# Order of scans, output product and gate in the state-space stage of a hybrid kernel

## The chip, the cores and the metric

The kernel runs on one core of a Trainium2 chip. The metric is the device time of one execution in microseconds, from runs on the chip; lower is better. The core has a matmul engine (TensorE, PE in the profile, with its weight loads shown as PEld), a vector engine (VectorE, DVE), a scalar engine for activations (ScalarE, ACT), a general engine (GpSimd, POOL) and a queue for DMAs (SyncE, SP). Each engine runs its own queue of instructions, and they synchronize by semaphores.

## The reference

Sixteen sequences of 512 tokens, 128 channels wide, pass through four residual layers: attention, a mixture of experts, a state-space layer, and the mixture of experts again. Only the state-space layer matters here. Cut to what counts:

```
zxbcdt = layernorm(x) @ in_proj_w.T        # z: 256, x: 256, B: 128, C: 128, dt: 32 heads
z, xBC, dt = split(zxbcdt);  dt = softplus(dt + dt_bias);  A = -exp(A_log)
xBC = silu(causal_conv4(xBC) + conv_b);  X, B, C = split(xBC)
# chunks of 32 tokens, 32 heads of 8 channels, state of 128
Y_diag = C B^T * exp(segsum(A dt)) applied to X dt          # within a chunk
states = B, decay to the chunk's end, X dt                  # one state per chunk
states = scan over the 16 chunks with the chunk decays
Y_off  = C applied to the state before the chunk, * exp(cumsum(A dt))
y = Y_diag + Y_off
y = layernorm(y) * ln_w * silu(z)
x = x + y @ out_proj_w.T
```

## The kernel before

The whole of `x` stays in on-chip memory. The stage runs over the sequences b = 0 to 15 (`ssm_pairs` writes out the first and last two and loops over pairs between them). Every engine has a function `batch(b, par, left)`, whose order of calls is written out by hand; it is the order of that engine's queue. `left` is the number of sequences still to come, capped at 2, and `has_before(b)` holds for all but b = 0. Within one `batch(b)` an engine does parts of three sequences: b itself, the output of b - 1, and the projections of b + 1 (with the layer norm of b + 2).

The 32 heads are taken in 8 groups of 4 (`SG` = 8). The steps named below:

- `diff(b, g)` (TensorE, L1640 to L1642): the log decays of head group g in PSUM bank g % 2. `exp_diff` (ScalarE, L1992) takes their exponential into a ring of four `decay` tiles. `mix(b, g)` (VectorE, L1838) multiplies by C B^T. `in_chunks(b, g)` (TensorE, 32 matmuls at L1668) multiplies with X and writes into banks 2 and 3.
- `fills` (TensorE, L1655) makes the chunk states in banks 6 and 7, and `fill_out` (ScalarE, L2001) copies them to `state`. `scan(b, part)` (VectorE, two instructions at L1846 for each of the parts 0 to 3) runs the recurrence over chunks. Part 0 waits for all of `fill_out`; the last scan raises `scanned`.
- `in_proj(b + 1, ..., q, back)` (TensorE, L1572 to L1574, three matmuls): convolution tap `back` of the projection of block q (0 and 1 are X, 2 is B, 3 is C), into bank 4 + q. So B goes to bank 6 and C to bank 7.
- `gate(b)` (TensorE, L306 to L308, 12 matmuls): the projection of z, into banks 0 and 1. `silu_z(b)` (ScalarE, L2017) applies Silu and raises `z_done`.
- `y_turn(b - 1)` (TensorE, L1675) transposes the previous y into banks 6 and 7, `y_copy` (ScalarE, L2010) copies it out and raises `yt_done`. `out_proj(b - 1)` (TensorE, 16 matmuls at L1682) writes the output product into bank 7. `out_add(b - 1)` (VectorE, four instructions at L1856) adds it to `x` and raises `x_done`.
- `shift_vector(b + 2)` (VectorE, L1359) makes the layer norm's shift; `norm(b + 2)` (ScalarE, four instructions at L1929) waits for it. In ScalarE's queue the order is `exp_diff(7)`, `y_copy(b - 1)`, `norm(b + 2)`, `silu_z(b)`, then `silu_x(b + 1, q)` (L1945).
- `from_state(b)` (TensorE, L1703 and L1706): C times the state, into banks 0 and 1. It waits for `z_done` and for `scanned`. After it comes `y_join(b)` (VectorE, L1866 and L1874), and with it the head of the next sequence.

The order at the end of a sequence on TensorE:

```python
                in_chunks(b, SG - 2)
                if has_before(b):
                    out_proj(b - 1)
                in_chunks(b, SG - 1)
                gate(b, par)
```

Of the kernel before, what the change touches and what calls it, by code (L numbers as in the profile page):

```python
# [35 lines left out]
TAPS, CH = 4, 32  # L36
# [37 lines left out]
def program(nc, x_in, out, w, x_slot, y_tok, phases):  # L74
    ctx = ExitStack()
    with ctx:
# [227 lines left out]
        def mm3(pe, o, a_h, a_l, b_h, b_l):  # L304

            pe.matmul(o, a_h, b_h, start=True, stop=False)  # L306
            pe.matmul(o, a_l, b_h, start=False, stop=False)
            return pe.matmul(o, a_h, b_l, start=False, stop=True)  # L308
# [366 lines left out]
        def has_before(b):  # L675
            return not (isinstance(b, int) and b == 0)
# [870 lines left out]
        FILLS = NC // 2  # L1547
# [10 lines left out]
        def ssm_tensor(pe, ph):  # L1558
# [8 lines left out]
            def in_proj(b, par, q, back):  # L1567
                k = TAPS - 1 - back
                c = slice(q * P, (q + 1) * P)
                o = bank[4 + q][:, :]  # L1570
                h, l = [x_pad[par][:, i, TAPS - back:TAPS - back + L] for i in range(2)]
                pe.matmul(o, wx_h[:, k, c], h, start=(back == 0), stop=False)  # L1572
                pe.matmul(o, wx_l[:, k, c], h, start=False, stop=False)
                last = pe.matmul(o, wx_h[:, k, c], l, start=False, stop=(back == TAPS - 1))  # L1574
                if back == TAPS - 1:
                    last.then_inc(s["xbc_mm"], 1)
# [7 lines left out]
            def sums(b):  # L1584
                pe.wait_ge(s["a_done"], b + 1)
                pe.wait_ge(s["act_x"], b * XB + 2)
                for c in range(CT):
                    last = pe.matmul(bank[5][:, :].rearrange("p (t c h) -> p c t h", t=QT, c=CT)[:, c, :, :],
                                     in_chunk[:, c, :], a_tok[:, :, :], start=True, stop=True)
                last.then_inc(s["tot_mm"], 1)  # L1590
                pe.matmul(bank[4][:, 0:P], later[:, :], flat_t(a_tok), start=True, stop=True)
                pe.matmul(bank[4][:, P:2 * P], until[:, :], flat_t(a_tok), start=True, stop=True).then_inc(s["dec_mm"], 1)
# [67 lines left out]
            def in_chunks(b, g):  # L1660
                if g == 0:
                    pe.wait_ge(s["xd_act"], b + 1)
                    pe.wait_ge(s["xd_dve"], b + 1)
                pe.wait_ge(s["mix_done"], b * SG + g + 1)
                for t in range(QT):
                    for c in range(CT):
                        o = bank[2 + t // 2][c * CH:(c + 1) * CH, (t % 2) * DI + g * CH:(t % 2) * DI + (g + 1) * CH]
                        last = pe.matmul(o, decay[:, g % D_RING, t, c, :], x_diag[:, t, c, g, :], start=True, stop=True)  # L1668
                last.then_inc(s["yd_mm"], 1)

            def y_turn(b):
                pe.wait_ge(s["y_zmul"], b + 1)
                for q in range(DI // P):
                    for t in range(QT):
                        last = pe.transpose(bank[6 + q][:, t * P:(t + 1) * P], y[:, t, q * P:(q + 1) * P], ident[:, :])  # L1675
                last.then_inc(s["yt_mm"], 1)
# [9 lines left out]
            def gate(b, par):  # L1686
                pe.wait_ge(s["diff_exp"], b * SG + SG)
                for t in range(QT):
                    c = slice(t * P, (t + 1) * P)
                    last = mm3(pe, bank[t // 2][:, (t % 2) * DI:(t % 2 + 1) * DI], xh[par][:, c], xl[par][:, c],  # L1690
                               wz_h[:, 0:DI], wz_l[:, 0:DI])
                    if t % 2:
                        last.then_inc(s["z_mm"], 1)
# [15 lines left out]
            def batch(b, par, left):  # L1709
                sums(b)  # L1710
                turns(b)
                rows(b, par, left)
                b_and_c(b)
                for g in range(SG):
                    diff(b, g)
                    if 2 <= g < 2 + QT:
                        fills(b, g - 2)
                    if left:
                        if g == 0:
                            pe.wait_ge(s["e_done"], b * 2 + 2)  # L1720
                        if g == TAPS:
                            pe.wait_ge(s["tot_done"], b + 1)
                        in_proj(b + 1, 1 - par, g // TAPS, g % TAPS)
                    if g >= 2:
                        in_chunks(b, g - 2)
                    if g == 6 and has_before(b):
                        pe.wait_ge(s["fill_out"], b * FILLS + FILLS)
                        y_turn(b - 1)
                in_chunks(b, SG - 2)
                if has_before(b):  # L1730
                    out_proj(b - 1)
                in_chunks(b, SG - 1)
                gate(b, par)
                if left:
                    if not has_before(b):
                        pe.wait_ge(s["fill_out"], FILLS)
                    for back in range(TAPS):
                        in_proj(b + 1, 1 - par, 2, back)
                    if has_before(b):
                        pe.wait_ge(s["x_done"], ph * SEQS + b)  # L1740
                    for back in range(TAPS):
                        in_proj(b + 1, 1 - par, 3, back)
                from_state(b)
                if left > 1:
                    pe.wait_ge(s["act_x"], (b + 1) * XB + 3)
                    ln_turn_wide(b + 2)
# [15 lines left out]
        def ssm_vector(dve, ph):  # L1762
# [70 lines left out]
            def mix(b, g):  # L1833
                if g == 0:
                    dve.wait_ge(s["cb_done"], b + 1)
                dve.wait_ge(s["diff_exp"], b * SG + g + 1)
                m = decay[:, g % D_RING, :, :, :].rearrange("p t c l -> p (t c l)")
                dve.tensor_tensor(m, m, cb[:, :], ALU.mult).then_inc(s["mix_done"], 1)  # L1838

            def scan(b, part):  # L1840
                if part == 0:
                    dve.wait_ge(s["fill_out"], b * FILLS + FILLS)
                    dve.wait_ge(s["tot_done"], b + 1)
                for x in range(2 * part, 2 * part + 2):
                    line = state[:, x, :, :].rearrange("p h c -> p (h c)")
                    last = dve.tensor_tensor_scan(line, e_tot[:, :, :].rearrange("p h c -> p (h c)"), line, 0.0, ALU.mult,  # L1846
                                                  ALU.add)
                if part == HP // 2 - 1:
                    last.then_inc(s["scanned"], 1)

            def out_add(b):
                dve.wait_ge(s["so_mm"], b + 1)
                dve.wait_ge(s["y_pow"], b + 1)
                for t in range(QT):
                    xt = tile_x(b * QT + t)
                    last = dve.scalar_tensor_tensor(out=xt, in0=bank[7][:, t * D:(t + 1) * D], scalar=y_rstd[:, t:t + 1],  # L1856
                                                    in1=xt, op0=ALU.mult, op1=ALU.add)
                last.then_inc(s["x_done"], 1)
# [19 lines left out]
            def batch(b, par, left):  # L1878
                scale_x(b)
                cumt_low(b)  # L1880
                cum_low(b)
                if left:
                    dt_in(b + 1)
                spread_x(b)
                if has_before(b):
                    y_moments(b - 1)
                if left:
                    dt_inverse(b + 1)
                mix(b, 0)
                mix(b, 1)  # L1890
                if has_before(b):
                    y_gate(b - 1)
                mix(b, 2)
                if left > 1:
                    ln_stats_vector(dve, SEQS + b + 2, b + 2)
                mix(b, 3)
                mix(b, 4)
                mix(b, 5)
                scan(b, 0)
                scan(b, 1)  # L1900
                mix(b, 6)
                scan(b, 2)
                mix(b, 7)
                scan(b, 3)
                if left > 1:
                    shift_vector(dve, b + 2)
                if has_before(b):
                    out_add(b - 1)
                y_join(b)
                if left > 1:  # L1910
                    ln_lo_wide_vector(dve, b + 2, par)
# [465 lines left out]
```

## Time and profile before

| | |
|---|---|
| runs, median of 3 | 2785.82 us (2782.82 to 2787.51) |
| profiled execution, its own time | 2776.01 us |
| its span | 2774.2 us |
| state-space stage, about | 1530 to 2294 us of the span |
| mean granted TensorE clock | 0.905 |
| TensorE / VectorE / ScalarE / GpSimd busy | 88% / 71% / 53% / 47% |

In the rows of a timeline the first number is the start in us from the span's start and the second how long the group took; engine, line, operation, the tile written and those read, the shape and the count follow. In brackets stands how long the engine had been idle before, and which engine, tile and line ended that wait. Instructions of an engine overlap a little at their ends, and the ends of matmuls are modelled. PEclk is the granted clock of TensorE: 1.00 is 2.4 GHz and 0.50 is 1.2 GHz. A sequence is here counted from the start of its `from_state`, so the stretch from 1703.5 to 1749.6 us ends with that of sequence 4.

### The profile page before, as it was taken

The numbers are of one execution on the slowest core, as the hardware profiler recorded it, in microseconds if no ns is written. First come the engines' busy times: TensorE is split into PE (matmuls) and PEld (weight loads), VectorE is DVE, ScalarE is ACT, GpSimd is POOL, SyncE is SP. The second block draws the span as 40 slices with busy tenths as digits, with TensorE's granted clock in tenths as the row PEclk, the third lists the DMA queues.
The fourth block names the chain that finished last, engine by engine and source line by source line (L and its number), as shares of the span: only waits on it lengthen the run. The fifth ranks groups of instructions, "written<-read, shape, count | busy, mean of one in ns | idle before, by whom it ended". The sixth has DMA issues, their size and how long they took to land.

```text
span 2774.2 us, 62048 instructions
## 1 busy us (share of the span) xinstructions
PE 2428.7 (88%) x21968; PEld 1784.7 (64%) x21968; DVE 1959.3 (71%) x5809; ACT 1469.9 (53%) x2778; POOL 1296.4 (47%) x1816
## 2 busy tenths in 40 slices
PE   4999999999999969979974999999999977988991
PEld 3666555665556548868863666666667656886881
DVE  3887888878888748856656566676666657885666
ACT  1555555555555546645552556565555646654550
POOL 0444455445544437766652324242333305774661
PEclk9999999999999986769996899999989987768996
DMA  7443444334443301113332000000000000112336
GB/s 161 63 59 49 59 59 59 56 51 59 59 59 53 42 29 47 47 56 89 91 100 83 2 2 2 2 2 2 2 2 2 2 2 29 48 51 78 91 89 192
DMA packets 118421, 140.68 MB, mean 51 GB/s; under 512 B 21452, under 2 KB 79953, under 8 KB 118000
## 3 DMA queue, kind: packets, MB, share of 16 engines
q1 hardware_dynamic: 101232, 102.68, 19.9%
q0 software_dynamic: 16896, 34.12, 3.6%
q8 instruction: 181, 2.97, 0.5%
q14 instruction: 112, 0.92, 0.1%
HBM read 45.85 MB, written 40.54 MB: 31 GB/s over the span
## 4 chain that ended last, share of the span: by engine, by line
PE 52%; DVE 19%; issue 10%; POOL 9%; ACT 7%; DMA 2%; SPq 1%; DVEq 0%; POOLq 0%; ACTq 0%
DVE state L1846 4%; POOL probs_t L562 3%; PE psum L1655 3%; POOL acc L568 3%; PE psum L476 3%; PE psum L1219 3%; DVE x_sb L1393 3%; PE psum L543 2%; PE psum L582 2%; PE psum L1193 2%; PE psum L1194 2%; PE psum L1703 2%; PE psum L1195 2%; PE psum L653 2%; DVE psum L485 2%
## 5 line engine op out<-in xcount | busy, mean ns | idle before, releaser
L485 DVE CUSTOM_DVE_ANT_0 psum<-psum,causal 128x512 f32<-128x512 f32 (+3 forms) x1024 | 481.7, 512 | 148.6 <-PE psum L476 145.5
L553 ACT ACTIVATE probs_t<-psum 128x512 f32<-128x512 f32 (+1 forms) x768 | 388.8, 523 | 356.8 <-PE psum L543 355.8
L562 POOL TENSOR_SCALAR_AFFINE_SELECT probs_t<-probs_t 128x256 f32<-128x256 f32 x512 | 189.8, 407 | 455.8 <-ACT probs_t L553 455.8
L1328 POOL DMA_INDIRECT y_tok<-yb,xb x272 | 265.8, 977 | 161.8 <-issue 128.0
L476 PE MATMUL psum<-ls,qs 96*128 96x512 f32 (+3 forms) x1024 | 323.8, 359 | 10.0 <-DVE mx_raw L485 6.3
L543 PE MATMUL psum<-qs,ls 98*128 98x512 f32 (+3 forms) x1024 | 311.9, 348 | 4.4 <-ACT probs_t L553 2.4
L476 PEld LDWEIGHTS psum<-ls,qs 96*128 96x128 f32 x1024 | 182.5, 194 | 185.3 <-DVE mx_raw L485 88.4
L996 POOL DMA_INDIRECT x_slot<-pay,pos_i x256 | 254.2, 993 | 93.3 <-issue 74.3
L2071 POOL TENSOR_SCALAR dt_r<-dt_v 128x128 f32<-128x128 f32 x16 | 9.2, 576 | 438.5 <-DVE dt_v L1767 438.5
L543 PEld LDWEIGHTS psum<-qs,ls 98*128 98x128 f32 x1024 | 177.7, 192 | 42.4 <-ACT probs_t L553 29.1
L1292 DVE TENSOR_TENSOR bh<-psum,bs 128x512 f32<-128x512 f32 x136 | 94.1, 692 | 139.2 <-ACT bs L1254 135.2
L601 PE MATMUL psum<-probs_t,lat_tok 128*32 128x512 f32 (+3 forms) x2048 | 177.8, 443 | 0.0
L568 POOL TENSOR_TENSOR acc<-probs_t 128x512 f32<-128x512 f32 x128 | 163.9, 1281 | 10.7
L1846 DVE TENSOR_TENSOR_SCAN state<-e_tot,state 128x512 f32<-128x512 f32 x128 | 148.7, 1212 | 20.7 <-ACT state L2001 20.7
L1838 DVE TENSOR_TENSOR decay<-decay,cb 128x512 f32<-128x512 f32 x128 | 95.1, 756 | 87.8 <-ACT decay L1992 87.8
L1254 ACT ACTIVATE bs<-psum 128x512 f32<-128x512 f32 x136 | 81.3, 598 | 136.7 <-PE psum L1195 136.7
L1219 PE MATMUL psum<-w_d,ht_h 128*128 x544 | 143.8, 341 | 1.2 <-DVE ht_l L1297 1.2
L2001 ACT ACTIVATE state<-psum 128x512 f32<-128x512 f32 (+1 forms) x128 | 120.0, 1046 | 45.3 <-PE psum L1655 45.3
L485 DVE DVE_READ_ACCUMULATOR2_ANT mx_raw<- 128x1 f32 x1024 | 142.4, 139 | 0.3
L1221 PE MATMUL psum<-w_d,ht_l 128*128 x544 | 121.4, 223 | 0.0
L1193 PE MATMUL psum<-w_gu_h,xt_h 128*128 x272 | 120.9, 444 | 0.2 <-issue 0.2
L1992 ACT ACTIVATE decay<-psum 128x512 f32<-128x512 f32 x128 | 74.5, 595 | 83.7 <-PE psum L1642 81.9
(336 smaller groups left out, 6805.5 us busy)
## 6 DMA issues: line engine op xcount, KB each, us to landing
qs<-q_h SPq DMA_DIRECT2D x96, 256.0 KB, 5.4
xb<-x_slot SPq DMA_DIRECT2D x272, 66.0 KB
y<-y_tok SPq DMA_DIRECT2D x32, 512.0 KB, 3.5
qs<-q_l SPq DMA_DIRECT2D x48, 256.0 KB, 5.6
qs<-r_h SPq DMA_DIRECT2D x32, 256.0 KB, 6.2
y_tok<-yb,xb POOLq DMA_INDIRECT x272
x_sb<-in_x SPq DMA_DIRECT2D x16, 256.0 KB, 5.4
qs<-r_l SPq DMA_DIRECT2D x16, 256.0 KB, 5.7
```

The lines of the kernel that those rows point to most:

```text
L476: last = pe.matmul(o[:, at:at + w_q], qs[0:3 * LD, h, qt * P:(qt + 1) * P], ls[b % 2][0:3 * LD, 0:w_q], start=(at == 0), stop=True, skip_g ...
L485: last = dve.tensor_tensor_reduce(out=bank[n % 3][:, at:at + w_q], in0=bank[n % 3][:, at:at + w_q], in1=causal[:, L - w_q:L], scale=1.0, s ...
L543: last = pe.matmul(o[:, at:at + L - kb * P], ls[b % 2][0:3 * LD + 2, kb * P:(kb + 1) * P], qs[0:3 * LD + 2, h, kb * P:L], start=(at == 0), ...
L553: act.activation(probs_t[:, i % 2, h % HG, UNIT_AT[k]:UNIT_AT[k] + UNIT_COLS[k]], bank[3 + m % 2][:, 0:UNIT_COLS[k]], ACT.Exp).then_inc(s[ ...
L562: last = pool.affine_select(out=p[:, :, at:at + P], in_=p[:, :, at:at + P], compare_op=ALU.is_ge, fill=0.0, base=0, pattern=[[0, 2], [1, P ...
L568: pool.tensor_tensor(acc[:, heads, :], p[:, :, 768:1024], p[:, :, 1024:1280], ALU.add).then_inc(s["p_step"], 1)
L601: last = pe.matmul(bank[5][j * LD:(j + 1) * LD, kb * P:L], lat_tok[b % 2][:, kb, :], probs_t[:, i % 2, j, at:at + L - kb * P], start=(kb = ...
L996: pool.indirect_dma_start(out=x_slot[f][:, :], out_offset=bass.IndirectOffsetOnAxis(ap=pos_i[slot][:, k, t:t + 1], axis=0), in_=pay[slot][ ...
L1193: pe.matmul(o, xt_h[par][:, c], w_h, start=True, stop=False)
L1219: pe.matmul(o, ht_h[par][:, m * P:(m + 1) * P], flat_d[c][:, bass.ds(at[k], 2 * D)], start=(k == 0 and c == 0), stop=False, skip_group_che ...
L1328: pool.indirect_dma_start(out=y_tok[f][:, :], out_offset=bass.IndirectOffsetOnAxis(ap=xb[:, j2, k, D:D + 1].bitcast(I32), axis=0), in_=yb[ ...
L1846: last = dve.tensor_tensor_scan(line, e_tot[:, :, :].rearrange("p h c -> p (h c)"), line, 0.0, ALU.mult, ALU.add)
```

## The change

On TensorE, the gate and the projection of B for the next sequence now come before the output product of the previous sequence; the last `in_chunks` follows the output product, and the projection of C follows that. The projection of B gets a wait for `yt_done`, because it overwrites bank 6, from which `y_copy` reads. The projection of C still waits for `x_done`, because it overwrites bank 7.

On VectorE, the last two `mix` come before all scans, `out_add` comes between scan 1 and scan 2, and the shift between scan 2 and scan 3.

```diff
@@ ssm_tensor, batch
                 in_chunks(b, SG - 2)
-                if has_before(b):
-                    out_proj(b - 1)
-                in_chunks(b, SG - 1)
                 gate(b, par)
                 if left:
-                    if not has_before(b):
+                    if has_before(b):
+                        pe.wait_ge(s["yt_done"], b * 2)
+                    else:
                         pe.wait_ge(s["fill_out"], FILLS)
                     for back in range(TAPS):
                         in_proj(b + 1, 1 - par, 2, back)
+                if has_before(b):
+                    out_proj(b - 1)
+                in_chunks(b, SG - 1)
+                if left:
                     if has_before(b):
                         pe.wait_ge(s["x_done"], ph * SEQS + b)
                     for back in range(TAPS):
@@ ssm_vector, batch
                 mix(b, 5)
+                mix(b, 6)
+                mix(b, 7)
                 scan(b, 0)
                 scan(b, 1)
-                mix(b, 6)
+                if has_before(b):
+                    out_add(b - 1)
                 scan(b, 2)
-                mix(b, 7)
-                scan(b, 3)
                 if left > 1:
                     shift_vector(dve, b + 2)
-                if has_before(b):
-                    out_add(b - 1)
+                scan(b, 3)
                 y_join(b)
```

## Rows read from the trace of the kernel before

**Rows 1.** The page, part 1: busy time and share of each engine.
```profile
...
PE 2428.7 (88%) x21968; PEld 1784.7 (64%) x21968; DVE 1959.3 (71%) x5809; ACT 1469.9 (53%) x2778; POOL 1296.4 (47%) x1816
```

**Rows 2.** Busy time by stretch, from one `from_state` to the next; sequences 5 and 6.
```profile
...
core 0: us, PE busy (x) PEld busy (x) DVE busy (x) ACT busy (x) POOL busy (x), PEclk, DMA share, GB/s
...
1749.60:1799.50 49.90, 46.63 (x635) 33.44 (x634) 31.53 (x63) 27.95 (x48) 15.89 (x25) 0.90 0.01 2
1799.50:1845.30 45.80, 42.30 (x638) 31.03 (x637) 32.09 (x63) 28.13 (x48) 16.94 (x25) 1.00 0.01 2
```

**Rows 3.** Timeline of TensorE's matmuls at the end of sequence 4.
```profile
...
1737.87 0.46 PE L1668 MATMUL psum<-x_diag,decay 128*32 128x32 f32 x32
...
1739.15 0.46 PE L1668 MATMUL psum<-x_diag,decay 128*32 128x32 f32 x32 [0.83 <-DVE decay L1838]
1739.54 2.05 PE L1682 MATMUL psum<-w_out,y_ch 128*128 128x128 f32 x16
...
1741.99 0.46 PE L1668 MATMUL psum<-x_diag,decay 128*32 128x32 f32 x32 [0.39 <-DVE decay L1838]
1742.38 0.39 PE L306 MATMUL psum<-wz_h,x_pad 128*128 128x256 f32 x1
...
1743.91 0.40 PE L1572 MATMUL psum<-x_pad,wx_h 128*128 128x512 f32 x1
...
1749.58 0.40 PE L1706 MATMUL psum<-x_dec,zero 128*32 128x256 f32 x1
```

**Rows 4.** Timeline of VectorE over the same stretch.
```profile
...
1733.95 4.57 DVE L1846 TENSOR_TENSOR_SCAN state<-e_tot,state 128x512 f32<-128x512 f32 x4 [1.31 <-ACT state L2001]
1738.43 0.67 DVE L1838 TENSOR_TENSOR decay<-decay,cb 128x512 f32<-128x512 f32 x1
1739.02 2.34 DVE L1846 TENSOR_TENSOR_SCAN state<-e_tot,state 128x512 f32<-128x512 f32 x2
...
1741.85 2.33 DVE L1846 TENSOR_TENSOR_SCAN state<-e_tot,state 128x512 f32<-128x512 f32 x2
1744.10 0.14 DVE L1359 SCALAR_TENSOR_TENSOR shift<-mv,rstd 128x4 f32<-128x4 f32 x1
1744.15 1.12 DVE L1856 SCALAR_TENSOR_TENSOR x_sb<-psum,y_rstd,x_sb 128x128 f32<-128x128 f32 x4
1753.95 1.29 DVE L1866 TENSOR_TENSOR y<-psum,e_cum 128x512 f32<-128x512 f32 x2 [8.67 <-PE psum L1703]
```

**Rows 5.** Timeline of ScalarE over the same stretch.
```profile
...
1737.28 0.60 ACT L1992 ACTIVATE decay<-psum 128x512 f32<-128x512 f32 x1 [2.17 <-PE psum L1642]
1737.77 1.08 ACT L2010 ACTIVATE y_ch<-psum 128x512 f32<-128x512 f32 x2
1744.28 1.65 ACT L1929 ACTIVATE xn<-x_sb,shift,rstd 128x128 f32<-128x128 f32 x4 [5.42 <-DVE shift L1359]
...
1747.24 1.09 ACT L2017 ACTIVATE z_s<-psum 128x512 f32<-128x512 f32 x2
```

**Rows 6.** TensorE in sequence 3: timeline around its longest wait, and the stretch behind it.
```profile
...
1671.62 0.50 PE L1640 MATMUL psum<-cum_t,sel 128*128 128x512 f32 x1 [2.08 <-ACT decay L1992]
...
1672.71 2.08 PE L1655 MATMUL psum<-x_dec,b_tok 32*128 32x256 f32 x8
...
1672.00:1679.00 7.00, 7.00 (x51) 4.02 (x51) 5.94 (x17) 3.10 (x5) 6.20 (x12) 0.51 0.02 4
```

**Rows 7.** Timelines of sequence 0 and of sequence 15.
```profile
...
1543.99 0.60 ACT L1992 ACTIVATE decay<-psum 128x512 f32<-128x512 f32 x1 [1.35 <-PE psum L1642]
...
1558.47 0.40 PE L1706 MATMUL psum<-x_dec,zero 128*32 128x256 f32 x1
...
2267.23 0.60 ACT L1992 ACTIVATE decay<-psum 128x512 f32<-128x512 f32 x1 [2.27 <-PE psum L1642]
...
2275.63 0.40 PE L1706 MATMUL psum<-x_dec,zero 128*32 128x256 f32 x1 [1.81 <-ACT z_s L2017]
...
2286.56 1.97 PE L1675 MATMUL psum<-ident,y 128*128 128x128 f32 x8 [6.56 <-DVE y L1829]
```

More of the change, by code:

```diff
@@ L1729, in batch @@
                 in_chunks(b, SG - 2)
+                gate(b, par)
+                if left:
+                    if has_before(b):
+                        pe.wait_ge(s["yt_done"], b * 2)
+                    else:
+                        pe.wait_ge(s["fill_out"], FILLS)
+                    for back in range(TAPS):
+                        in_proj(b + 1, 1 - par, 2, back)
                 if has_before(b):
@@ L1732, in batch @@
                 in_chunks(b, SG - 1)
-                gate(b, par)
                 if left:
-                    if not has_before(b):
-                        pe.wait_ge(s["fill_out"], FILLS)
-                    for back in range(TAPS):
-                        in_proj(b + 1, 1 - par, 2, back)
                     if has_before(b):
```

## The prediction

> **What bounds the kernel now.** I first read the busy shares: TensorE is busy for 88% of the span [rows 1], so time is lost wherever it waits. The change touches only the state-space stage, so I next cut that stage at the start of `from_state` of each sequence [rows 2]. Two things are to be seen. Sequence 6 takes 45.8 us with a granted clock of 1.00 throughout, sequence 5 takes 49.9 us with 0.90, and such pairs repeat through the stage. And TensorE is busy for 42.3 of the 45.8 us: it sets the pace, with a few waits in it.
>
> Then I read one sequence (number 4) instruction by instruction, once per engine, over its last 12 us, because all moved work lies there. On TensorE [rows 3] the order is `in_chunks(5)`, a wait of 0.83 us, `in_chunks(6)`, `out_proj` of the sequence before, a wait of 0.39 us, `in_chunks(7)`, the gate, the projection of B and of C, `from_state`. Both waits are for `mix` on VectorE. VectorE [rows 4] runs scans 0 and 1 (4.57 us), `mix(6)`, scan 2, `mix(7)`, scan 3, `shift_vector` at 1744.10, `out_add`; ScalarE [rows 5] sits idle for 5.42 us until that shift, normalizes, loads a table, and applies Silu to the gate. This is so in sequences 1 to 13, which have both a sequence before and a layer norm to make. So three chains run towards `from_state` at 1749.58: TensorE's own matmuls arrive at about 1749.5, Silu of the gate at 1747.24 + 1.09 = 1748.33, and the scans at 1741.85 + 2.33 = 1744.2. TensorE arrives last, with 1.2 us over Silu and 5.4 us over the scans. After `from_state` everything waits for it, VectorE for 8.67 us [rows 4], so what delays `from_state` delays the sequence.
>
> **The change part by part**, on the times of sequence 4. No instruction is added or removed: 128x512 products, scans and matmuls only change places, no DMA moves, and SyncE's and GpSimd's queues are untouched (GpSimd's step sizes for the next sequence are made ahead of this tail).
>
> *The last two mixes.* `mix(6)` waits for the exponential 6 and runs while VectorE now idles or scans. `mix(7)` waits for exponential 7, which ends at 1737.28 + 0.60 = 1737.88 [rows 5] and cannot come sooner, since `diff(7)` is reached on TensorE without a wait on VectorE. It takes 0.67 us, so it ends at 1738.6. But all scans now stand behind it: they began at 1733.95 and will begin at about 1738.55. That is 4.6 us of scanning pushed back; the two mixes (1.2 us) are what is taken from between the scans in return. On TensorE the two waits of 0.83 and 0.39 us go.
>
> *TensorE's new order.* `in_chunks(5)` starts at 1737.87, each `in_chunks` takes 0.39 us (1741.99 to 1742.38), so the gate starts at 1738.65. It takes 1743.91 - 1742.38 = 1.53 us, to 1740.2. B's projection is 12 of the 24 matmuls between 1743.91 and 1749.5, so 2.79 us, to 1743.0; the wait that it gets, `yt_done`, is met at 1737.77 + 1.08 = 1738.85, so it costs nothing (were it late, C's projection would cover it only until the wait below). `out_proj` (2.05 us) ends at 1745.0, `in_chunks(7)` at about 1745.3. C's projection waits for `out_add`, because both use bank 7.
>
> *`out_add` between the scans.* Scans 0 and 1 end at 1738.55 + 4.57 = 1743.1. `out_add` needs `out_proj`, which is only done at 1745.0: VectorE stands for 2.0 us, with scan 2, the shift and scan 3 queued behind it. It then runs from 1745.1 to 1746.2 (1.12 us [rows 4]); scan 2 (2.33 us) ends at 1748.5, the shift starts at 1748.4, scan 3 ends at 1750.8. C's projection runs from 1746.3 to 1749.1, so TensorE has waited 1.0 us there.
>
> That VectorE does not let a ready scan pass a waiting instruction is what the 2.0 us rest on. The rows agree: scan 2 had its data when the last `fill_out` was copied, before 1733.95, and started only behind `mix(6)`, at 1739.02. The Trainium skill states it as a rule that speaks against this edit (page "TensorE: Matmul & The Clock Gate", section "Architectural detail: the array is 16× 32×32, not 1× 128×128"): ScalarE and VectorE run strictly first in, first out. With it the sequence loses what follows; without it scan 2 and the shift would come some 2 us earlier and lose about 1 us in place of 3.
>
> *What is late next: the shift.* It moves from 1744.10 to 1748.4, 4.3 us later. From the shift to the end of Silu of the gate ScalarE takes 1748.33 - 1744.10 = 4.23 us (norm 1.65, table, two Silu; Silu of x_t is queued behind), all in one queue, so the early gate on TensorE buys nothing: Silu ends at 1752.6. `from_state` waits for it, since it writes the gate's banks: 1752.7 in place of 1749.58, **3.1 us later**. Before it TensorE waits for 1752.7 - 1749.1 = 3.6 us.
>
> Sum at full clock. Sequences 1 to 13 have all of this: 13 x 3.1 = 40.3. Sequence 0 has no `out_add`: exponential 7 ends at 1544.59 [rows 7], four scans follow, the shift starts near 1552.0 and Silu ends at 1556.2; `from_state` comes at 1556.3 in place of 1558.47, a gain of 2.1. Sequence 14 has no shift, and only the scans bind: 1750.8 against 1749.6, +1.2. In sequence 15 exponential 7 ends at 2267.83, scans 0 and 1 at 2273.0, `out_add` at 2274.1, scan 3 at 2278.7, against 2275.63: +3.1. Together **+42.5 us**.
>
> *The clock.* The rows show a price for making TensorE wait. Behind a wait of 2.08 us in sequence 3 the granted clock was 0.51 for 7 us, that is the 1.2 GHz level, and eight 256-column matmuls took 2.08 us [rows 6]. This happens in every second sequence, after waits of this size. Between 1749.6 and 1799.5 the clock reads 0.90 over 49.9 us: 10 us at the low level, for 49.9 - 45.8 = 4.1 us, or 0.41 us per low us [rows 2]. The new wait of 3.6 us is longer than the one that drops the clock half of the time, and shorter than the one of 6.56 us near the end, behind which eight transposes took 1.97 us [rows 7]. What follows it, `from_state` and the head, is pure TensorE work. Bounds: nothing, if the clock holds; or a whole further fall of 10 us at 0.41 in 13 sequences, 53 us. I take a fall in each, 7 to 8 us long with about 3 us inside the wait itself, so 4.5 us on work: 13 x 4.5 x 0.41 = **24 us**. I leave the old falls as they are.
>
> The Trainium skill's rule for the price (page "TensorE: Matmul & The Clock Gate", section "Terms") is half of the time at the low level; by it this term would be 13 x 4.5 x 0.5 = 29 us. The rows show less, because other engines hide a part.
>
> Sum: 42.5 + 24 = 66.5 us. On the profiled execution, 2776.0 us (span 2774.2 and 1.8 around it), that gives 2842.5. The median of the runs, 2785.8, lies 9.8 above it, so the forecast is **2852 us**.
>
> **Rivals.**
>
> A, the stalls without a further fall of the clock: the new wait replaces one fall by another, or the old ones shift away. For it: sequences with waits of 2 us hold 1.00 half of the time. Against it: the wait is 1.5 us longer. 2785.8 + 42.5 = 2828, down to about 2810 if some of the seven old falls (4 us each) go.
>
> B, the heavy case: a fall in the new wait that lasts through `from_state` and the head in each sequence (53 us), and the old ones with it in more than half. 2785.8 + 42.5 + 53 = 2881, up to 2905.
>
> C, faster: TensorE sets the pace, and the edit works as a removal of the two mix waits, 1.22 us in each of 15 sequences, plus 2 us in sequence 0: about -20 us, 2766. That needs the shift to Silu chain not to end last. It decides where the shift starts: up to 1745.3 (1.2 us later than now) `from_state` loses nothing. By the rows even an `out_add` that never waits gives 1743.1 + 1.1 + 2.3 = 1746.5, so the case needs one of my durations on VectorE or the queue order to be wrong.
>
> D, no change: the waits removed and the ones added cancel, if `out_proj` were early and the shift near 1745.3.
>
> **How the numbers follow.** The forecast's own case, 2838 to 2866, has 0.45; A 0.25; B 0.22; C 0.05; D 0.03. A change within 0.2% (5.6 us) is about what a measurement of this kernel cannot tell from none. C gives faster 0.05, D same 0.03, the rest slower 0.92. Leaving out C and D, the upper end of B and the lower end of A gives 2812 to 2890.
>
> **What the profile after should show.** The wait of `xn` for the shift grows from 5.4 to about 9.7 us in 13 sequences; `out_add` has a wait of 2 us on `out_proj`; the 0.83 and 0.39 us before `in_chunks` are gone; `from_state` has a wait of 3.6 us on `z_s`, and C's projection one of 1 us on `out_add`. Sequences at a clock of 1.00, if there are any, take 49 us. The clock reads low behind the wait, in `from_state`. The prediction is wrong if the shift starts before 1745.3 on this scale, or wrong in size if the clock shows no fall there or a longer one.

## The result and the profile after

| | before | after |
|---|---|---|
| median of the runs | 2784.32 us (2772.41 to 2787.51, 4 runs) | 2817.89 us (2803.89 to 2819.86, 4 runs) |
| ratio | | 1.0114, 95% interval 1.0084 to 1.0145 |
| profiled execution | 2776.01 us | 2819.86 us |
| TensorE busy | 88% | 86% |

The change costs 33.6 us by the medians. 66.5 us were forecast: the sign is right, and the size is twice too large. The range holds the time only because it was drawn wide enough for rival A (2810 to 2828); the forecast's own case (2838 to 2866) does not. The ratios count only executions within 1.5% of the fastest of their kernel, which leaves some out in e4 alone.

The page of the changed kernel, part 1, answers to [rows 1]. TensorE has the same work in a longer span:

```profile
...
PE 2425.5 (86%) x21968; PEld 1785.6 (63%) x21968; DVE 1961.0 (70%) x5809; ACT 1470.8 (52%) x2778; POOL 1289.0 (46%) x1816
```

The end of sequence 4 in the changed kernel corresponds to [rows 3] to [rows 5]. Exponential 7 starts at 1748.04 here and at 1737.28 before, so 10.76 us have to be taken off for a comparison. First VectorE's timeline:

```profile
...
1748.67 0.69 DVE L1841 TENSOR_TENSOR decay<-decay,cb 128x512 f32<-128x512 f32 x1 [2.08 <-ACT decay L1995]
1749.28 4.57 DVE L1849 TENSOR_TENSOR_SCAN state<-e_tot,state 128x512 f32<-128x512 f32 x4
1755.65 1.13 DVE L1859 SCALAR_TENSOR_TENSOR x_sb<-psum,y_rstd,x_sb 128x128 f32<-128x128 f32 x4 [1.80 <-PE psum L1682]
1756.69 2.33 DVE L1849 TENSOR_TENSOR_SCAN state<-e_tot,state 128x512 f32<-128x512 f32 x2
1758.93 0.14 DVE L1359 SCALAR_TENSOR_TENSOR shift<-mv,rstd 128x4 f32<-128x4 f32 x1
1758.99 2.33 DVE L1849 TENSOR_TENSOR_SCAN state<-e_tot,state 128x512 f32<-128x512 f32 x2
```

`mix(7)` is followed by scans 0 and 1, then VectorE stands for 1.80 us until `out_proj` is done, adds, and comes to the shift only at 1758.93, which is 10.89 us after exponential 7. Before, it was 6.82 us. ScalarE:

```profile
...
1748.04 0.60 ACT L1995 ACTIVATE decay<-psum 128x512 f32<-128x512 f32 x1 [2.18 <-PE psum L1642]
...
1759.11 1.65 ACT L1932 ACTIVATE xn<-x_sb,shift,rstd 128x128 f32<-128x128 f32 x4 [9.49 <-DVE shift L1359]
...
1762.07 1.08 ACT L2020 ACTIVATE z_s<-psum 128x512 f32<-128x512 f32 x2
```

It waits 9.49 us for that shift in place of 5.42 us, and the second Silu ends at 1762.07 + 1.08 = 1763.15. TensorE (gate, `out_proj`, projection of C, `from_state`):

```profile
...
1749.33 0.39 PE L306 MATMUL psum<-wz_h,x_pad 128*128 128x256 f32 x1
...
1753.66 1.95 PE L1682 MATMUL psum<-w_out,y_ch 128*128 128x128 f32 x16
...
1756.83 0.50 PE L1572 MATMUL psum<-x_pad,wx_h 128*128 128x512 f32 x1 [0.83 <-DVE x_sb L1859]
...
1763.21 0.40 PE L1706 MATMUL psum<-x_dec,zero 128*32 128x256 f32 x1 [3.32 <-ACT z_s L2020]
```

`from_state` starts 0.06 us after Silu, 15.17 us after exponential 7, against 12.30 us before. The list of waits (from 1558.5 to 2280 us) shows the same in 13 or 14 sequences:

```profile
...
ACT xn L1932 <- DVE shift L1359: 123.3, 13, 9.5
...
PE psum L1706 <- ACT z_s L2020: 46.2, 14, 3.3
...
DVE x_sb L1859 <- PE psum L1682: 25.2, 14, 1.8
```

So the structure is as predicted. The clock is not. Stretches from one `from_state` to the next in the changed kernel, for sequences 4 to 7, beside [rows 2]:

```profile
...
core 0: us, PE busy (x) PEld busy (x) DVE busy (x) ACT busy (x) POOL busy (x), PEclk, DMA share, GB/s
1714.60:1763.20 48.60, 42.12 (x634) 31.27 (x634) 32.27 (x63) 28.10 (x48) 16.05 (x25) 0.97 0.01 2
1763.20:1812.80 49.60, 43.38 (x634) 31.60 (x634) 31.90 (x63) 28.12 (x48) 16.27 (x25) 0.96 0.01 2
1812.80:1863.90 51.10, 44.87 (x634) 32.93 (x634) 31.66 (x63) 28.02 (x48) 16.08 (x25) 0.90 0.01 2
1863.90:1919.50 55.60, 49.37 (x634) 35.46 (x634) 31.65 (x63) 27.95 (x48) 15.44 (x25) 0.81 0.01 2
```

Each of sequences 1 to 14 now has some low clock, for 2 to 22 us: the stretches read 0.97, 0.96, 0.90, 0.81 over four in a row, where in the kernel before every second sequence has none.

**A table by parts.** I cut each sequence in three at events that every timeline has: the head, from the start of `from_state` to that of exponential 0; the middle, to exponential 7; the tail, to the next `from_state`. The sums below run over sequences 1 to 14 (counted, as ahead, by the `from_state` that ends them), in the profiled execution of each kernel. A middle at a clock of 1.00 takes 17.2 us in all kernels whose head is not edited, so 14 of them make 241. In e8 to e13 exponential 0 is moved forward, so their heads are shorter and their middles longer by the cut alone: with e11 to e13 a middle at 1.00 takes 20.4 to 20.5 us, and 14 make 286; e8 and e9 have none at 1.00. The last column counts the sequences in whose middle the clock falls, before exponential 7. Each row is one execution; how much another one of the same kernel can differ is seen in e4.

| kernel | head | middle | tail | falls in the middle |
|---|---|---|---|---|
| before | 227.0 | 272.6 | 173.3 | 7 |
| after | 223.9 | 273.9 | 210.4 | 9 |
| e1, VectorE's part | 228.1 | 302.0 | 183.8 | 14 |
| e2, TensorE's part | 226.6 | 276.9 | 179.2 | 10 |
| e3, shift ahead of the addition | 226.8 | 303.6 | 186.8 | 14 |
| e4, mixes one scan earlier | 224.6 | 298.3 | 156.8 | 13 |
| e5, shift last | 225.2 | 326.8 | 239.4 | 14 |
| e6, wait filled | 225.0 | 263.7 | 210.4 | 8 |
| e8, exponentials first, on before | 177.2 | 391.6 | 164.6 | 14 |
| e9, the same on after | 178.4 | 394.8 | 210.4 | 14 |
| e11, short head wait, on before | 177.5 | 335.6 | 169.5 | 9 |
| e12, the same on after | 177.4 | 319.0 | 210.4 | 6 |
| e13, short head wait and mixes | 175.6 | 295.5 | 160.3 | 2 |

Before to after: head -3.1, middle +1.3, tail +37.1 us. Sequence 15 adds 3.3 us (44.39 to 47.67), and the first `from_state` comes 2.3 us sooner after exponential 7 of sequence 0 (14.48 to 12.23). That makes 36.3 us of the 43.8 us between the two profiled executions. The rest lies outside the edited stretch and is no effect of the change as far as can be seen: exponential 0 of sequence 0 starts at 1524.6 us before and 1528.6 after, and at 1516.3 in e9, with the same instructions ahead of it. The 33.6 us of the medians come close to the 36.3 us of the parts, but four executions of one kernel lie up to 16 us apart, so that closeness proves little; the parts do.

### The profile page after: what moved, and what is told of

Read it like the earlier page. It is cut to its first block, busy times and chain, and to the rows that moved or that the text cites. A ratio compares the mean times of both kernels' runs of the same rounds, so it can differ in the third digit from the quotient of the medians.

```text
span 2818.1 us, 62048 instructions
## 1 busy us (share of the span) xinstructions
PE 2425.5 (86%) x21968; PEld 1785.6 (63%) x21968; DVE 1961.0 (70%) x5809; ACT 1470.8 (52%) x2778; POOL 1289.0 (46%) x1816
## 4 chain that ended last, share of the span: by engine, by line
PE 41%; DVE 17%; POOL 17%; issue 14%; ACT 8%; DMA 2%; SPq 1%; POOLq 0%; DVEq 0%; ACTq 0%
POOL y_tok L1328 8%; POOL probs_t L562 3%; PE psum L1655 3%; POOL acc L568 3%; PE psum L476 3%; DVE x_sb L1393 3%; PE psum L582 2%; PE psum L543 2%; PE psum L653 2%; DVE psum L485 2%; PE psum L1703 2%; DVE xn L617 2%; ACT x_diag L1985 2%; PE psum L1572 2%; DVE state L1849 2%
## 5 line engine op out<-in xcount | busy, mean ns | idle before, releaser
L1572 PE MATMUL psum<-x_pad,wx_h 128*128 128x512 f32 x256 | 113.5, 443 | 11.6 <-DVE x_sb L1859 11.6
```

## The experiments

All ratios are to the kernel before, measured beside it on the same chip.

**e1: VectorE's part alone.** The order of VectorE is that of the change, the order of TensorE that of before. Against the changed kernel:

```diff
                 in_chunks(b, SG - 2)
+                if has_before(b):
+                    out_proj(b - 1)
+                in_chunks(b, SG - 1)
                 gate(b, par)
                 if left:
-                    if has_before(b):
-                        pe.wait_ge(s["yt_done"], b * 2)
-                    else:
+                    if not has_before(b):
                         pe.wait_ge(s["fill_out"], FILLS)
                     for back in range(TAPS):
                         in_proj(b + 1, 1 - par, 2, back)
-                if has_before(b):
-                    out_proj(b - 1)
-                in_chunks(b, SG - 1)
-                if left:
```

> Only VectorE's new order, TensorE's order as before. Theory (the shift leads to from_state through the normalization and Silu of the gate): the output product is early again, so the output addition waits for nothing and the shift starts about 2 us earlier than in the changed kernel. from_state then comes about 1.2 us later than before in 13 sequences, and scans cost 3 us in the last: about +12 to +16 us against the kernel before, under half of the change's +33. Rival (the loss is made by TensorE's new order alone): no change or a gain of some 15 us, since the two waits of 0.83 and 0.39 us for the mixes are gone.

Measured: 2815.30 us against 2785.93, ratio 1.0115 (1.0095 to 1.0135), about +29 us by the medians; the whole change has a ratio of 1.0114. By the parts, the theory of the tail holds: 13.26 us, +0.96 where 1.2 was expected. But the middle rose by 29 us. Head, middle and tail of its sequence 5 by stretches, columns as above:

```profile
...
1766.50:1782.60 16.10, 14.69 (x252) 11.36 (x252) 10.41 (x21) 10.95 (x22) 3.62 (x4) 0.89 0.00 1
1782.60:1804.30 21.70, 21.03 (x232) 13.36 (x233) 10.52 (x30) 11.55 (x17) 12.25 (x21) 0.76 0.01 3
1804.30:1817.50 13.20, 10.99 (x151) 8.89 (x149) 10.74 (x14) 5.59 (x11) 0.00 (x0) 1.00 0.01 1
```

The clock reads 0.76 over the middle, and it falls in all 14 sequences. So the mechanism expected was there with its size, and a second one that I had held fixed was twice as large. Both forecasts of the total missed.

**e2: TensorE's part alone.** The change without its edit of VectorE's order, against the changed kernel:

```diff
                 mix(b, 5)
-                mix(b, 6)
-                mix(b, 7)
                 scan(b, 0)
                 scan(b, 1)
-                if has_before(b):
-                    out_add(b - 1)
+                mix(b, 6)
                 scan(b, 2)
+                mix(b, 7)
+                scan(b, 3)
                 if left > 1:
                     shift_vector(dve, b + 2)
-                scan(b, 3)
+                if has_before(b):
+                    out_add(b - 1)
```

> Only TensorE's new order, VectorE's order as before. Theory: the shift keeps its place ahead of the output addition, so Silu of the gate is not late. What is left is that the projection of C waits about 1 us for the output addition, against 0.39 us saved before the last in_chunks: +0.2 to +0.5 us per sequence, +3 to +7 us in all. Rival (a wait of TensorE costs clock as forecast): +15 us or more, with low clock in stretches where it reads 1.00 before.

Measured: 2783.22 us, ratio 1.0000 (0.9980 to 1.0021). The tail is 12.75 us, +0.45 as expected. TensorE's part alone is worth nothing, and costs nothing that can be measured.

**e3: the shift ahead of the output addition.**

```diff
                 scan(b, 1)
+                if left > 1:
+                    shift_vector(dve, b + 2)
                 if has_before(b):
                     out_add(b - 1)
                 scan(b, 2)
-                if left > 1:
-                    shift_vector(dve, b + 2)
                 scan(b, 3)
```

> The changed kernel with the shift moved from behind scan 2 to ahead of the output addition. Theory: Silu of the gate ends about 5 us earlier and stops being the last; from_state then waits for the last scan, 1 to 1.2 us later than before. Total +12 to +18 us against the kernel before, so half of the loss goes, and the wait before from_state is named after the scan. Rival (the scans alone or the clock make the loss): it stays at +28 us or more.

Measured: 2812.78 us, ratio 1.0094 (1.0066 to 1.0122), +27 us. The tail fell from 15.16 to 13.35 us, and the wait before `from_state` (1.51 us) is now for the scan: that step is as expected. The start of `from_state` of its sequence 4:

```profile
...
1756.93 0.38 PE L1706 MATMUL psum<-x_dec,zero 128*32 128x256 f32 x1 [1.50 <-DVE state L1849]
```

The total is not: +12 to +18 us were expected. The 24 us gained in the tails, and more, went to the middle (+30 us against the changed kernel). Low clock in `from_state` is gone in this run, and the heads are no shorter for it (226.8 against 223.9 us), a first sign against the term for it.

**e4: the last two mixes one scan earlier, on the kernel before.**

```diff
                 scan(b, 0)
-                scan(b, 1)
                 mix(b, 6)
-                scan(b, 2)
+                scan(b, 1)
                 mix(b, 7)
+                scan(b, 2)
                 scan(b, 3)
```

> The kernel before with each of the last two mixes one scan part earlier (scan 0, mix 6, scan 1, mix 7, scans 2 and 3), nothing else. Theory: TensorE arrives last at from_state in the kernel before, so the two waits of 0.83 and 0.39 us are worth their length: about 1.1 us in each of 14 sequences, 15 to 20 us faster, with the shift's start unchanged. Rival (what is gained there is given back at the low clock or by a later wait): within 5 us of the kernel before.

Measured: six executions of 2730.79, 2759.53, 2780.80, 2782.02, 2787.71 and 2787.73 us; median 2781.41 against 2785.93. The mean granted clock is 0.914 and 0.902 in the first two, 0.890 to 0.894 in the others. The ratio, 0.9856 (0.9810 to 0.9901), rests on the first two alone; by the medians it is 0.998. The tail is 11.20 us, -1.10 as expected, in every sequence of the profiled execution (2780.80 us). Its sequences 4, 5 and 7:

```profile
...
1697.90:1742.80 44.90, 42.24 (x639) 31.04 (x638) 31.96 (x63) 28.11 (x48) 16.02 (x25) 1.00 0.01 2
1742.80:1790.00 47.20, 44.86 (x635) 32.53 (x634) 31.82 (x63) 28.08 (x48) 15.72 (x25) 0.93 0.01 2
1837.40:1889.20 51.80, 49.46 (x639) 34.91 (x642) 31.56 (x63) 27.98 (x48) 15.34 (x25) 0.84 0.01 2
```

A sequence whose clock holds takes 44.9 us; the others, with the same instructions, 47.2 and 51.8 us. Between the theory and its rival this is a draw: the 16 us are there, and in most executions the falls take them back. The middle of 298.3 us in the table belongs to one of the four longer executions. The fastest is 50 us shorter with a higher clock, and 50 us is nearly all that the falls cost in the profiled middles (298.3 - 241 = 57). So many falls are not a fixed property of this order of instructions; the fast executions have no profile.

**e5: the shift behind scan 3, in the changed kernel.**

```diff
                 scan(b, 2)
+                scan(b, 3)
                 if left > 1:
                     shift_vector(dve, b + 2)
-                scan(b, 3)
```

> The changed kernel with the shift one scan part later, behind scan 3. Theory (structure and the old falls are separate terms): the tail, from exponential 7 to the next from_state, is 15.16 us in the changed kernel and follows the shift one for one, so it becomes 17.4 us in sequences 1 to 13: +29 us against the changed kernel, give or take some 10 us by the falls behind the wait in the head. Rival (the scans or the clock bind the tail): the tail stays under 16 us.

Measured: 2887.22 us, ratio 1.0341 (1.0302 to 1.0381). The tail is 17.38 us, longer by the 2.2 us that scan 3 takes, which confirms the chain from the shift to `from_state` with another dose. TensorE's wait in the timeline:

```profile
...
2306.18 0.63 PE L1706 MATMUL psum<-x_dec,zero 128*32 128x256 f32 x1 [5.54 <-ACT z_s L2020]
```

The total is +63 us against the changed kernel by the two ratios, not +29. It is the middle again: 23.4 us on average over sequences 2 to 13 in place of 19.7, with a fall in each of them.

**e6: the wait filled with work.** C's projection is computed twice in sequences 1 to 13. The first pass is overwritten by the second; `count=False` makes it raise no semaphore.

```diff
                         pe.wait_ge(s["x_done"], ph * SEQS + b)
+                    if has_before(b) and left > 1:
+                        for back in range(TAPS):
+                            in_proj(b + 1, 1 - par, 3, back, count=False)
                     for back in range(TAPS):
                         in_proj(b + 1, 1 - par, 3, back)
```

> The changed kernel, computing the projection of C twice in sequences 1 to 13 (the first pass of 12 matmuls is overwritten), so that TensorE works through 2.8 of the 3.3 us in which it waits before from_state. Theory after the first runs (low clock in from_state costs nothing, because its matmuls take the same time at both levels): the low clock in from_state goes, the tail stays 15.1 to 15.3 us and the head about 15.8 us, so the time is that of the changed kernel within 10 us, whatever the falls in the middle do. Prediction's theory (falls behind the new wait cost 24 us): about 24 us faster than the changed kernel.

Measured: 2802.36 us, ratio 1.0066 (1.0039 to 1.0093), so some 13 us faster than the changed kernel by the two ratios, whose intervals overlap a little. The row of the wait before `from_state`, 46.2 us in the changed kernel:

```profile
...
PE psum L1706 <- ACT z_s L2023: 6.7, 13, 0.5
```

In its profile the clock is low in `from_state` only in sequence 0. Head and tail are 225.0 and 210.4 us against 223.9 and 210.4: removing the low clock there gave nothing. The 24 us that the prediction's theory wanted are not there. The gain stands in the middle, 263.7 against 273.9 us. It is a little over my bound of 10 us, and whether a denser tail makes the falls in the middle fewer, or this was the run's luck, one kernel does not tell.

**e8: exponentials 0 and 1 ahead of the spreading copies, on the kernel before.** The spreading copies (`spread_x`, L1982 on ScalarE) write X into the layout that `in_chunks` reads.

```diff
+                exp_diff(b, 0)
+                exp_diff(b, 1)
                 spread_x(b)
                 if left:
                     exp_dt(b + 1)
                 for g in range(SG):
-                    exp_diff(b, g)
+                    if g >= 2:
+                        exp_diff(b, g)
```

> The kernel before with exponentials 0 and 1 ahead of ScalarE's eight spreading copies, so that diff 2 on TensorE no longer waits 2.1 us for them in the head. Theory (the falls in the middle come from that wait): the clock reads 1.00 through the middle of nearly all sequences, which gives back the 36 us that the falls cost there, and each sequence is some 0.9 us shorter besides: 35 to 50 us faster than the kernel before. Rival (the falls come from the small matmuls of the middle itself): the clock falls as often, and the gain is under 15 us.

Measured: 2838.46 us, ratio 1.0186 (1.0157 to 1.0214), +51 us. I was wrong on the step "diff 2 no longer waits": the wait moved and grew. `mix(0)` stands on VectorE behind the inverse for dt, which waits for ScalarE's `exp_dt`, which waits behind the spreading copies. TensorE's row, and the stretch behind it:

```profile
...
1743.05 0.46 PE L1668 MATMUL psum<-x_diag,decay 128*32 128x32 f32 x32 [2.88 <-DVE decay L1838]
```

```profile
...
1745.00:1758.00 13.00, 13.00 (x171) 7.99 (x168) 6.69 (x17) 7.47 (x10) 8.61 (x17) 0.77 0.01 1
```

The wait is 2.88 us in place of 2.08, and the clock falls in all 14 sequences, for 6.8 to 23.9 us each.

**e9: the same edit as in e8, on the changed kernel.**

> The changed kernel with the same edit on ScalarE. Theory: the change's own structural cost stands free of the falls in the middle: tails of 15.2 against 12.3 us in 13 sequences, +0.9 and +3.0 in the last two, -2.3 in the first, some -3 in the heads, so 33 to 40 us slower than the run with the edit on the kernel before, with a spread of its runs that is smaller. Rival (the wait before from_state drops the clock for longer once the middle is dense): more than 50 us slower than that run.

Measured: 2889.47 us, ratio 1.0391 (1.0355 to 1.0426). That is 51 us over e8, where 33 to 40 were expected: the rival's number. But its mechanism is not what made it. On average over sequences 2 to 13 the tail is 15.16 against 11.85 us. e8's tail is 11.2 us, not the 12.3 us of before, in seven of its fourteen sequences: those in which the clock is low for over 20 us, up to exponential 7, so that TensorE reaches `in_chunks` late enough to find its mixes done. 12 x 3.31 = 40 us, the tails of sequences 1 and 14 add 6, sequence 15 adds 4, sequence 0 takes off 4, and heads and middles together add only 4. The expectation had taken 12.3 us for the tail.

**e11, e12, e13: a shorter wait in the head.** Exponentials 0 and 1 and `exp_dt` go ahead of ScalarE's spreading copies, and mixes 0 and 1 ahead of VectorE's moments and inverse: e11 on the kernel before, e12 on the changed one, e13 on e4. In the diff against the kernel before, other lines are left out:

```diff
@@ ssm_scalar, batch
+                exp_diff(b, 0)
+                exp_diff(b, 1)
+                if left:
+                    exp_dt(b + 1)
                 spread_x(b)
-                if left:
-                    exp_dt(b + 1)
                 for g in range(SG):
-                    exp_diff(b, g)
+                    if g >= 2:
+                        exp_diff(b, g)
@@ ssm_vector, batch
                 spread_x(b)
+                mix(b, 0)
+                mix(b, 1)
                 if has_before(b):
                     y_moments(b - 1)
                 if left:
                     dt_inverse(b + 1)
-                mix(b, 0)
-                mix(b, 1)
```

> The kernel before with exponentials 0 and 1 and the one for dt ahead of ScalarE's spreading copies, and mixes 0 and 1 on VectorE ahead of the moments and the inverse. In the run with the exponentials alone the wait in the head had only moved to the first in_chunks and grown from 2.1 to 2.9 us, with low clock in every sequence. Theory (the length of the longest wait in the head decides how often and how long the clock falls in the middle): the wait shrinks to about 1 us, falls become rare, the middle stays within 1 us of its full-clock length: 30 to 50 us faster than the kernel before. Rival (the small matmuls of the middle drop the clock by themselves): falls in most sequences and a gain under 15 us.

> The changed kernel with the same edit. Theory: without falls in the middle the change shows its structural cost alone: +2.86 us in 13 tails (37), +0.9 and +3.0 in the last two, -2.3 in the first, some -3 in the heads: 34 to 40 us slower than the run with the edit on the kernel before. Rival (the new wait before from_state carries a clock price of its own, as predicted): 50 us or more slower.

> The short head wait, with the last two mixes one scan part earlier, on the kernel before. Theory: the mixes take their 1.1 us off each tail as in their own run (11.2 against 12.3 us), and now no falls take it back: 13 to 18 us faster than the run with the head edit alone, 45 to 65 us faster than the kernel before. Rival (falls return with the shorter sequence): no faster than the head edit alone.

These three ran on a chip on which the kernel before takes 2950.38 us, so only ratios and differences are to be used. The extra time lies outside the state-space stage: from the first `from_state` to the last e11 takes 724.4 us here, and the kernel before took 717.2 us on the other chip, but the first one comes at 1641.5 us in place of 1558.5, and the last is followed by 575.6 us in place of 498.6.

| kernel | median us | ratio (95%) |
|---|---|---|
| e11 | 2936.45 | 0.9957 (0.9939 to 0.9975) |
| e12 | 2972.07 | 1.0067 (1.0040 to 1.0093) |
| e13 | 2901.02 | 0.9850 (0.9823 to 0.9876) |

e11 gained 14 us, not 30 to 50. The falls did not become rare: 9 sequences of 14 have one, behind waits of at most 1.1 us in head and middle. TensorE waits 0.9 us for the spreading copies and 1.1 us for `fill_out` a little later, so about 2 us together. Its waits from 1558.5 to 2231.2 us (total, times, longest):

```profile
...
PE psum L1655 <- ACT state L2001: 14.7, 13, 1.1
PE psum L1668 <- ACT x_diag L1982: 10.8, 13, 0.9
```

So the length of the longest wait does not decide it alone, and the theory fails. The rival's two numbers came true (falls in most sequences, a gain under 15 us), but not its mechanism: e13 has the same matmuls in its middle and two falls. Where e11's 14 us come from is not shown, as there is no profile of the kernel before on this chip.

e12 is 35.6 us slower than e11, inside the 34 to 40 expected, and that is luck. The expectation rested on middles without falls, and both have them. By parts, e12 against e11: tails +40.9 us, sequence 15 +4.1, sequence 0 -3.6, so 41 us of structure, a little more than expected because e11's tail is 11.2 us in four sequences. The middles give back 16.6 us (6 falls in place of 9), and 10 us more are lost ahead of exponential 7 of sequence 0. What e12 does show is the price of low clock in `from_state`: 12 of its 14 heads have some and e11's have none, and the heads take 177.4 and 177.5 us.

e13 is 35 us faster than e11, where 13 to 18 were expected, and **49 us faster than the kernel before**, the best version of this study (45 to 65 were expected). Its sequences 3 to 5:

```profile
...
1735.30:1785.90 50.60, 48.15 (x635) 34.71 (x634) 31.58 (x63) 29.08 (x50) 14.91 (x25) 0.87 0.01 2
1785.90:1830.50 44.60, 42.23 (x635) 31.04 (x634) 31.66 (x63) 26.73 (x46) 17.00 (x25) 1.00 0.01 2
1830.50:1875.00 44.50, 42.23 (x635) 30.85 (x634) 31.96 (x63) 27.90 (x48) 17.54 (x25) 1.00 0.01 2
```

From sequence 4 to 14 the clock holds, at 44.2 to 44.6 us each against 45.8 us at the same clock in [rows 2]. So some 1.4 us per sequence are structure, 20 us over 14 of them. Most of the rest of the 49 us is clock: by the table the falls in the middles cost 295.5 - 286 = 9 us here and 272.6 - 241 = 32 us in the kernel before.

## Why the prediction was wrong, step by step

**TensorE's queue: right.** The gate starts 1.29 us after exponential 7 (forecast 1.37), the wait for `yt_done` is met, C's projection waits 0.83 us (1.0), and the 0.83 and 0.39 us ahead of `in_chunks` are gone.

**`out_add` between the scans: right.** VectorE stands 1.80 us in front of it (2.0), and scan 2, which has its data, does not pass it. e1, where `out_proj` is early, has a tail of 13.26 us in place of 15.16.

**The shift is late next: right, and the decisive step.** It comes 4.07 us later (4.3), and `from_state` 2.87 us later (3.1). e3 moved the shift up and the tail shrank to the scans' bound, e5 moved it down by one scan part and the tail grew by 2.2 us.

**Sum at full clock: 42.5 forecast.** The pieces: sequences 1 to 13 have tails longer by 36.3 us in all, 2.8 us each (forecast 40.3); +0.9 in sequence 14 (1.2), +3.0 in the tail of 15 (3.1), -2.3 in sequence 0 (-2.1). Not forecast were heads shorter by 3.1 us in all. The sum is 35, so this term was 7 us too large: 4 us because the shift came 0.2 us sooner than forecast in each sequence and four tails of the kernel before were already 12.5 us and not 12.3, and 3 us by the heads.

**The clock: wrong, and this is the step that failed.** "I take a fall in each, 7 to 8 us long with about 3 us inside the wait itself, so 4.5 us on work: 13 x 4.5 x 0.41 = 24 us." A fall came with 12 of the 14 `from_state` of sequences 0 to 13, so that part was right. But it was 3.4 us long, of which 2.1 to 3.4 us lay on work, and above all it cost nothing. Two windows of the changed kernel, both from the start of `from_state` to its end, in a sequence without a fall there and in one with it:

```profile
...
1763.20:1767.40 4.20, 4.19 (x33) 1.81 (x34) 0.01 (x1) 1.75 (x4) 0.00 (x0) 1.00 0.00 0
1812.80:1816.90 4.10, 4.09 (x33) 2.29 (x34) 0.00 (x0) 1.71 (x3) 0.00 (x0) 0.60 0.00 0
```

33 matmuls (the 32 of `from_state` and the first behind them) take 4.19 us at a clock of 1.00 and 4.09 us at 0.60. I had priced low clock at 0.41 us per us from sequences 5 and 6, where it falls in the middle, and there the price holds: a middle is 1.4, 3.0, 4.5 and 7.5 us longer for 3.4, 6.8, 10.2 and 17.1 us of low clock, 0.44 us per us. I then used the price where other matmuls run. e6 confirms it by taking the low clock out of `from_state`: head and tail do not get shorter. So does the pair e11 and e12. With 35 + 0 in place of 42.5 + 24, rival A, the stalls without a price of the clock, names the mechanism that was found, and its 2828 is nearer to the measured 2818 than the forecast. The falls themselves did come, which A had not assumed.

The Trainium skill (page "TensorE: Matmul & The Clock Gate", section "Back-to-back issue gap") gives for an isolated matmul a spacing of the columns over the clock: for 256 columns 213 ns at the low level and 109 ns at the full one. The trace does not show this factor of two for the matmuls of `from_state`: the 32 starts lie within 3.43 us in the first window and 3.40 us in the second, about 110 ns apart in both. They are no isolated matmuls, since each lasts some 650 ns and they overlap. What holds them at this pace no run shows.

**"I leave the old falls as they are": right by its number, with luck.** The middles of before and after differ by 1.3 us, but in e1 and e3, which edit nothing that head or middle wait for, they grew by 29 and 31 us. That the change's own middle did not is not explained by anything in the prediction.

**What stays open:** what decides in which sequences the clock falls. The wait of 2.0 to 2.1 us in the head is the same in all sequences, and in the kernel before every second one has a fall behind it; e8's 2.88 us had one in each; e11 still had nine with its two shorter waits, e13 with the same head had two. The number of falls does not follow the length of the tail in one direction: the profiled executions with tails of 12.3 us have 7, of 11.2 us 13, of 13.3 us 14, of 15.2 us 9 or 8, of 17.4 us 14. And by e4 it is not even fixed by the program.

## What to carry to other kernels

When an engine's queue is reordered, follow the late instruction to the next engine's queue: here VectorE's wait for the late product cost time through the tiny shift queued behind it, which set the start of `from_state`. Price a lower clock by the rows of the very matmuls that will run under it. And where the clock falls in some repetitions of a loop and not in others, split the loop into parts and compare the parts: the totals of e1 and e3 alone would have led to the wrong cause, and e12's total agreed with its expectation by luck.

## What the runs showed of the hardware

- The matmuls of `from_state` (32-column weights, 256 columns moving) take the same time with the clock mostly at 1.2 GHz as at 2.4 GHz: 4.09 us at a mean clock of 0.60 and 4.19 us at 1.00 in the changed kernel. In the middle of a sequence low clock costs 0.44 us per us.
- One program's executions on one chip differed by 57 us (e4: 2730.79 to 2787.73 us), with mean clocks from 0.914 to 0.890.
- One chip took 2950.38 us for the kernel before, 6% more than the medians of 2785.93 and 2787.30 us on two others, and the extra time lay outside the state-space stage.
